# A layer-norm tail rebuilt: means from one scaled ScalarE pass, single tiles, two banks for the last tile, final steps on ScalarE and GpSimd

## The reference

```
h = gelu(x @ Wd + bd) @ Wu + bu          # 512 -> 256 -> 512
h = x + h
mean = h.mean(-1); var = ((h - mean)**2).mean(-1)
out = (h - mean) * rsqrt(var + 1e-5) * g + b   # g, b: rows of the sequence's expert
```

## Time and profile before

| | |
|---|---|
| median of 3 runs | 1041.93 us (1040.11 to 1042.93) |
| profiled execution | span 1039.0 us, from the first to the last instruction; the profile gives no other time of its own, and the median is 2.93 us above this span |
| busy share | PE 99%, PE weight loads 83%, DVE 76%, ACT 50%, POOL 1% |
| last matmul of the run starts | 1032.12 us |
| the last two stores are issued | from 1035.76 us |

### The profile page before, as it was taken

The page is one execution under the profiler, slowest core; times in us unless marked ns, Lnnn a source line. Parts: engine busy times, 40 slices in busy tenths (PEclk is TensorE's granted clock), DMA queues, the critical chain, the costliest instruction groups (busy, mean ns, idle before and its releaser), DMA issues.

```text
span 1039.0 us, 13809 instructions
## 1 busy us (share of the span) xinstructions
PE 1028.9 (99%) x4857; PEld 859.5 (83%) x4857; DVE 792.5 (76%) x1380; ACT 524.4 (50%) x955; POOL 7.5 (1%) x18
## 2 busy tenths in 40 slices
PE   8999999999999999999999999999999999999997
PEld 7899888888888878888889888888888887888886
DVE  5647957767598898887966796677668889887798
ACT  4336875454265443433565487554435644434357
POOL 0000000000000000000000000000000000000001
PEclk9999999999999999999999999999999999999999
DMA  8340211210133272521644122312004322423152
GB/s 205 60 183 21 95 48 41 82 41 21 61 144 121 101 201 83 159 85 49 238 120 118 58 68 82 122 41 81 21 21 162 142 81 104 157 98 109 41 163 81
DMA packets 91006, 101.61 MB, mean 98 GB/s; under 512 B 36830, under 2 KB 71738, under 8 KB 87098
## 3 DMA queue, kind: packets, MB, share of 16 engines
q1 hardware_dynamic: 90848, 100.71, 29.8%
q10 hardware_dynamic: 90, 0.02, 0.0%
HBM read 79.74 MB, written 20.97 MB: 97 GB/s over the span
## 4 chain that ended last, share of the span: by engine, by line
PE 59%; DVE 3%; ACT 1%; issue 1%; DVEq 0%; ACTq 0%
PE bank L224 20%; PE bank L225 20%; PE bank L226 20%; DVE acc L1124 0%; PE bank L462 0%; DVE z_last L1281 0%; DVE w_lo L1018 0%; DVE z_last L1290 0%; ACT gel L833 0%; DVE xp2l L1018 0%; ACT acc L810 0%; DVE hid_lo L1018 0%; ACT xp3h L586 0%; ACT e3h L586 0%; PE bank L376 0%
## 5 line engine op out<-in xcount | busy, mean ns | idle before, releaser
L224 PE MATMUL bank<-hid_hi,w_lo 128*128 128x512 f32 x512 | 200.3, 391 | 0.3
L676 ACT ACTIVATE sbc<-sbc,bias 128x512 f32<-128x512 f32 x112 | 80.5, 724 | 236.0 <-DVE sbc L1099 174.4
L225 PE MATMUL bank<-hid_hi,w_hi 128*128 128x512 f32 x512 | 199.3, 389 | 0.0
L226 PE MATMUL bank<-hid_lo,w_hi 128*128 128x512 f32 x512 | 199.2, 389 | 0.0
L1124 DVE TENSOR_TENSOR acc<-bank,acc 128x512 f32<-128x512 f32 x224 | 153.6, 686 | 50.9 <-PE bank L226 50.4
L224 PE MATMUL bank<-ta_hi,w_lo 128*128 128x512 f32 x448 | 174.8, 390 | 0.0
L226 PE MATMUL bank<-ta_lo,w_hi 128*128 128x512 f32 x448 | 174.4, 389 | 0.0
L225 PE MATMUL bank<-ta_hi,w_hi 128*128 128x512 f32 x448 | 174.3, 389 | 0.0
L1099 DVE TENSOR_TENSOR sbc<-bank,sbc 128x512 f32<-128x512 f32 x144 | 98.1, 686 | 38.8 <-PE bank L226 38.6
L586 ACT ACTIVATE sbc<-bank 128x512 f32<-128x512 f32 x112 | 66.4, 595 | 112.7 <-PE bank L226 112.5
L1018 DVE TENSOR_TENSOR w_lo<-w_raw,w_hi 128x256 fp32r<-128x256 f32 (+1 forms) x176 | 93.6, 562 | 37.0 <-ACT w_hi L586 37.0
(11 more groups left out here) (224 smaller groups left out, 1532.4 us busy)
## 6 DMA issues: line engine op xcount, KB each, us to landing
w_raw<-in_L_cond_mW SPq DMA_DIRECT2D x48, 512.0 KB, 3.4
w_raw<-in_L_cond_cW SPq DMA_DIRECT2D x32, 512.0 KB, 4.4
pre_d<-sbc SPq DMA_DIRECT2D x10, 1024.0 KB, 3.9
sbc<-pre_d SPq DMA_DIRECT2D x10, 1024.0 KB, 7.3
x_blk<-in_x SPq DMA_DIRECT2D x64, 64.0 KB, 2.3
e_raw<-in_L_cond_W_down SPq DMA_DIRECT2D x8, 512.0 KB, 4.5
e_raw<-in_L_cond_W_up SPq DMA_DIRECT2D x8, 512.0 KB, 4.1
proj_hi<-aw_hi SPq DMA_DIRECT2D x2, 1024.0 KB, 10.2
```

The source lines that it names most:

```text
L224: nc.tensor.matmul(dst, w_l, a_h, start=start, stop=False, **kw)
L225: nc.tensor.matmul(dst, w_h, a_h, start=False, stop=False, **kw)
L226: return nc.tensor.matmul(dst, w_h, a_l, start=False, stop=stop, **kw)
L676: nc.scalar.activation(dst, dst, ACT.Gelu, **kw).then_inc(g_done[key], 1)
```

## The change

Seven edits, all in the last layer's end. (1) ACT's first pass multiplies by -1/512 and accumulates straight into `nmean`; the Copy is gone. (2) PE works pair 3 by single tiles. (3) Tile (1,3) goes to two banks, 3 and 4, its left 256 columns in one and its right 256 in the other, with twelve matmuls of 256 columns in place of six of 512. (4) DVE takes the statistics of that tile by halves, and centres and finishes it by halves. (5) Tiles (0,2) and (1,2) get their last step elsewhere: ACT multiplies by rstd (`act_scale`), POOL adds b (`finish`). (6) `veps` and `rstd` have a column of their own for each of these tiles, and the DVE order becomes (0,2), (0,3), (1,0), (1,1), (1,2), (1,3). (7) SP stores (0,3) ahead of (0,2); the right half of (1,3) is stored from ACT's queue, the left half and then (1,2) from SP's.

```diff
+                split = n == 2 * NBAT - 1 and t == TT - 1
+                if split:
+                    pe.wait_ge(z_cent, 4 * n - 3)
                 for k in range(KT):
+                    bank = ps[LAST_BANK[k // 2]] if split else ps[b0 + t]
...
+                halves = tuple(zip(LAST_BANK, (0, V // 2), (V // 2, V)))
+                for bank, c0, c1 in halves if n == 2 * NBAT - 1 and t == TT - 1 else ((b0 + t, 0, V),):
+                    for m in range(MT):
+                        w = slice(m * V + c0, m * V + c1)
+                        last = mm3(ps[bank][:, c0:c1], ...)
+                    last.then_inc(up_mm, 1)
+            if n == 2 * NBAT - 1:
+                groups = tuple((t,) for t in range(TT))
...
+        def act_scale(act, pp, t):
+            n = 2 * NBAT - 2 + pp
+            act.wait_ge(z_cent, 4 * n + t + 1)
+            act.wait_ge(rstd_done, R_NO[(pp, t)])
+            nc.scalar.activation(z_tile(n, t), z_tile(n, t), ACT.Identity, scale=rstd_last[:, column(pp, t)])\
+                .then_inc(scaled, 1)
...
-                nc.scalar.activation(sjunk[:, c, 0, :], bank, ACT.Identity, accum_out=ssum[:, col]).then_inc(sum_done, 1)
-                act.wait_ge(sum_done, c + 1)
-                nc.scalar.activation(nmean[:, col], ssum[:, col], ACT.Copy, scale=-1.0 / V).then_inc(nmean_done, 1)
+                nc.scalar.activation(sjunk[:, c, 0, :], bank, ACT.Identity, scale=-1.0 / V,
+                                     accum_out=nmean[:, col]).then_inc(nmean_done, 1)
...
+                if c >= 2 and c != 3:
+                    act_scale(act, 0 if c == 2 else 1, 2)
...
             act_expert_last(act)
+            act.wait_ge(half_done, 2)
+            store_last(act, 1, TT - 1, RIGHT)
...
+            for t in (0, 1):
                 dve_eps_last(dve, 1, t)
                 dve_cent_last(dve, 1, t)
                 dve_out_last(dve, 1, t)
+            dve_half_stats(dve, 0)
+            dve_eps_last(dve, 1, 2)
+            dve_cent_last(dve, 1, 2)
+            dve_half_stats(dve, 1)
+            dve_aggr_last(dve, TT - 1)
+            dve_cent_halves(dve, TT - 1)
+            dve_out_last(dve, 1, 3, LEFT)
+            dve_out_last(dve, 1, 3, RIGHT)
...
+            def finish(c, pp, t):
+                n = 2 * NBAT - 2 + pp
+                pool.wait_ge(scaled, c)
+                nc.gpsimd.tensor_tensor(z_tile(n, t), z_tile(n, t), ln_p[n][:, t // TS, 1, :], ALU.add).then_inc(pool_done, 1)
+            power(0, 2)
+            power(0, 3)
+            power(1, 0)
+            finish(1, 0, 2)
+            power(1, 1)
+            power(1, 2)
+            power(1, 3)
+            finish(2, 1, 2)
...
+            sp.wait_ge(half_done, 1)
+            store_last(sp, 1, 3, LEFT)
+            sp.wait_ge(pool_done, 2)
+            store_last(sp, 1, 2, FULL)
```

More of the change, by code:

```diff
@@ L95, in build @@
         mhalf = sb("mhalf", [P, TT])
-        ssum = sb("ssum", [P, 2 * TT])
+        stat_last = sb("stat_last", [P, 2, 6])
+        veps_last = sb("veps_last", [P, 2 * TT])
+        rstd_last = sb("rstd_last", [P, 2 * TT])
         nmean = sb("nmean", [P, 2 * TT])
@@ L203, in build @@
             "max_done", "nmax_done", "rinv_done", "probs_done"))
-        sum_done, nmean_done, ssq_done = sem("sum_done"), sem("nmean_done"), sem("ssq_done")
+        nmean_done, ssq_done, half_done, pool_done = (sem(n) for n in ("nmean_done", "ssq_done", "half_done", "pool_done"))
+        scaled = sem("scaled")
         st_done, ag_done, ve_done, rstd_done, z_cent = (sem(n) for n in (
@@ L460, in token_tile @@
                 pe.wait_ge(xb_done, 4 * n + 4)
+                split = n == 2 * NBAT - 1 and t == TT - 1
+                if split:
+                    pe.wait_ge(z_cent, 4 * n - 3)
                 for k in range(KT):
-                    nc.tensor.matmul(ps[b0 + t][:, k * P:(k + 1) * P],
-                                     acc[:, k, pp * TB + t * P:pp * TB + (t + 1) * P], ident[:, :],
-                                     is_transpose=True, start=k == 0, stop=True, skip_group_check=True)
+                    bank = ps[LAST_BANK[k // 2]] if split else ps[b0 + t]
+                    nc.tensor.matmul(bank[:, k * P:(k + 1) * P], acc[:, k, pp * TB + t * P:pp * TB + (t + 1) * P],
+                                     ident[:, :], is_transpose=True, start=k == 0 or split and k == 2, stop=True,
+                                     skip_group_check=True)
             def up_tile(t):
@@ L470, in up_tile @@
                 pe.wait_ge(e_l, 8 * bb + E_RANK[bb][4 * pp + 2 + s] + 1)
[L471 to L477, removed]
+                halves = tuple(zip(LAST_BANK, (0, V // 2), (V // 2, V)))
+                for bank, c0, c1 in halves if n == 2 * NBAT - 1 and t == TT - 1 else ((b0 + t, 0, V),):
+                    for m in range(MT):
+                        w = slice(m * V + c0, m * V + c1)
+                        last = mm3(ps[bank][:, c0:c1], t_hi3[:, m, tok], t_lo3[:, m, tok], u_hi[:, s, w],
+                                   u_lo[:, s, w], False, True, skip_group_check=True)
+                    last.then_inc(up_mm, 1)
+            if n == 2 * NBAT - 1:
+                groups = tuple((t,) for t in range(TT))
+            elif bb + 1 < NBAT:
+                groups = (range(TT),)
+            else:
+                groups = ((0, 1), (2, 3))
+            for tiles in groups:
                 for t in tiles:
@@ L1258, in dve_norm @@
                         .then_inc(z_done[pp], 1)
-        R_TILE = ((0, 2), (0, 3), (1, 0), (1, 1), (1, 3), (1, 2))
-        R_NO = {pt: 4 * NBAT - 3 + c + 1 for c, pt in enumerate(R_TILE)}
+        L_TILE = A_STAT + ((1, 3),)
+        R_NO = {pt: 4 * NBAT - 3 + c + 1 for c, pt in enumerate(L_TILE)}
+        column = lambda pp, t: slice(TT * pp + t, TT * pp + t + 1)
         def dve_eps_last(dve, pp, t):
[L1264 to L1276, removed]
@@ new lines, in dve_eps_last, with dve_half_stats @@
+            dve.wait_ge(ssq_done, A_NO[(pp, t)] + 1)
+            nc.vector.tensor_scalar(veps_last[:, column(pp, t)], ssq[:, column(pp, t)], 1.0 / V, LN_EPS, ALU.mult, ALU.add)\
+                .then_inc(ve_done, 1)
+        FULL, LEFT, RIGHT = slice(0, V), slice(0, V // 2), slice(V // 2, V)
+        HALF = tuple(zip(LAST_BANK, (LEFT, RIGHT)))
+        def dve_half_stats(dve, h):
+            bank, cols = HALF[h]
+            dve.wait_ge(up_mm, 8 * NBAT + h)
+            nc.vector.bn_stats(stat_last[:, h, :], ps[bank][:, cols]).then_inc(st_done, 1)
@@ L1278, in dve_cent_last, with dve_aggr_last @@
+        def dve_aggr_last(dve, t):
+            seen = 8 * NBAT - 6
+            dve.wait_ge(st_done, seen + 2)
+            nc.vector.bn_aggr(mv[:, t, :], stat_last[:, :, :]).then_inc(ag_done, 1)
+            dve.wait_ge(ag_done, seen + 1)
+            nc.vector.tensor_scalar_add(veps_last[:, column(1, t)], mv[:, t, 1:2], LN_EPS).then_inc(ve_done, 1)
         def dve_cent_last(dve, pp, t):
             n = 2 * NBAT - 2 + pp
-            mean = nmean[:, TT * pp + t:TT * pp + t + 1] if (pp, t) in A_NO else mv[:, t, 0:1]
@@ L1281, in dve_cent_last @@
[L1281 to L1286, removed]
+            nc.vector.scalar_tensor_tensor(out=z_tile(n, t), in0=ps[(0 if pp else 4) + t][:, :], scalar=nmean[:, column(pp, t)],
+                                           in1=ln_p[n][:, t // TS, 0, :], op0=ALU.add, op1=ALU.mult).then_inc(z_cent, 1)
@@ new lines, in dve_cent_halves, with out_last @@
+        def dve_cent_halves(dve, t):
+            n = 2 * NBAT - 1
+            for bank, cols in HALF:
+                nc.vector.scalar_tensor_tensor(out=z_tile(n, t)[:, cols], in0=ps[bank][:, cols], scalar=mv[:, t, 0:1],
+                                               in1=ln_p[n][:, t // TS, 0, cols], op0=ALU.subtract, op1=ALU.mult)\
+                    .then_inc(z_cent, 1)
+        def out_last(engine, pp, t, cols):
+            n = 2 * NBAT - 2 + pp
+            return engine.scalar_tensor_tensor(out=z_tile(n, t)[:, cols], in0=z_tile(n, t)[:, cols],
+                                               scalar=rstd_last[:, column(pp, t)], in1=ln_p[n][:, t // TS, 1, cols],
+                                               op0=ALU.mult, op1=ALU.add)
@@ L1287, in dve_out_last @@
+        def dve_out_last(dve, pp, t, cols=FULL):
             n = 2 * NBAT - 2 + pp
             dve.wait_ge(rstd_done, R_NO[(pp, t)])
[L1289 to L1292, removed]
+            dve.wait_ge(z_cent, 4 * n + t + (2 if cols is RIGHT else 1))
+            out_last(nc.vector, pp, t, cols).then_inc(z_done[pp] if cols is FULL else half_done, 1)
@@ L1310, in dve_norm_last @@
-            for t in (3, 2):
+            dve_eps_last(dve, 0, 2)
+            dve_cent_last(dve, 0, 2)
+            dve_eps_last(dve, 0, 3)
+            dve_cent_last(dve, 0, 3)
+            dve_out_last(dve, 0, 3)
+            dve.wait_ge(ln_in[1], 64 * NBAT)
+            for t in (0, 1):
                 dve_eps_last(dve, 1, t)
-            for t in (2, 3):
```

(34 more changed lines are left out.)

14 lines of the change are left out of this document (1 added, 13 removed).

## The result

The changed kernel takes 1042.87 us (median of 21 runs, 1041.43 to 1043.88) against 1041.51 for the kernel before (21 runs, 1039.77 to 1042.93): ratio 1.0014, 95% interval 1.0008 to 1.0020. It is slower by 0.14% (the medians lie 1.36 us apart), where 0.3 us less was forecast. The profiled execution has a span of 1040.1 us and took 1041.87.

The account below looks back on a forecast made before the run. PE, busy 99% of the 1039.0 us span, bounds the run; only DVE's tail could move. Of 1.5 us off DVE some 0.6 remained, the last add and stores left 0.3: span 1038.7, median 1041.6, range 1040.1 to 1043.8.

Parts of the forecast that it names:

- the forecast case: Whole kernel: span 0.3 us shorter, at 1038.7, median 1041.6; chance 0.48.
- rival A: Last tiles: POOL's add shuts out DVE's final steps reading two SBUF tensors; span 1040.3, median 1043.2; chance 0.34.
- DVE's load: DVE's last tiles: two final steps fewer, halves added; 1.5 us less work, some 0.6 left after waits for ACT.
- Copy: ACT's statistics passes: without it, squaring starts 0.71 after summing instead of 0.95; a tile costs 1.39 instead of 1.63.
- POOL's add: POOL's bias add on (0,2) and (1,2), 128x512 with two inputs: taken as 1.2 us, shown by no row.
- The second way to the end: Kernel's end: POOL's add on (1,2) ends at 1035.95, 0.13 later than the right half, and sets the end.
- Rival B: POOL's add takes 1.9 us, delaying (1,1)'s power and all behind it; span 1039.9, median 1042.8; chance 0.08.
- ACT waits: DVE waits 0.3 us for ACT's sum of squares before (0,3), and 0.3 before (1,1).
- Rival C: Nothing gained: ACT's scaled pass or SBUF reads are slower and waits eat the rest; 1041.9; chance 0.10.
- Scaling pass: ACT's multiplication of (0,2) by rstd, reading SBUF with a pointer column, costs 0.63 us.
- PE: PE's last pair by single tiles, last tile in halves: the split costs nothing, but would with DVE a microsecond earlier.
- Halves on VectorE: Last tile's statistics, centring and final step by halves: three extra starts of 0.15 each, 0.45 us on.

Follow-up runs that it names:

- e2: Changed kernel with GpSimd's two adds replaced by memsets of 1472 columns of unused memory; span 1039.2 us, 17.57 from ScalarE's last-pair bias pass to the end.
- e3: Changed kernel with tiles (1,0) and (1,3) centred in place in their PSUM banks; span 1038.1 us, ratio 0.9991 to the kernel before.
- m1: Kernel before with 200 adds of 128x128 on GpSimd from 580.4 us on; span 1044.7 us.
- e7: e3 with GpSimd's second add on (1,1) instead of (1,2), (1,2) centred in its bank and finished by VectorE, stores by readiness; ratio 0.9995 to the kernel before.
- e8: e6 with SP's last stores in the order in which they are ready; span 1039.5 us, 18.24 from ScalarE's last-pair bias pass to the end.
- e6: Changed kernel with VectorE doing (0,2)'s and (1,2)'s final steps, no ScalarE scaling or GpSimd add; span 1039.3 us, 18.68 from last-pair bias pass to end.

## Why the prediction was wrong

The median fell in the range and in the band of no measurable change at 0.3%, but the direction was wrong, and the forecast case with it; rival A, given 0.34, is what happened.

The step that failed is in *DVE's load*, "(1,0): ... final step 1029.72, free 1030.39", and the same step for (1,3), "left half at 1034.94, right at 1035.34". Both priced a final step at its length from the kernel before, though each now runs beside an instruction that the trace before never had beside it. Measured: 1.66 instead of 0.75, and 1.83 instead of 0.87. I had named the meeting as rival A and priced it as 1.3 us, span 1040.3 (measured 1.30 and 1040.1), and given it less weight because no row showed it. That the two figures agree so well is luck: rival A has VectorE done at 1037.75, 16.69 after the bias pass, where 1035.29 + 1.83 - 1020.86 = 16.26 was measured, and the end 2.55 after that, where it was 2.98. The two errors, 0.43 each, cancel. A trace in which the two never overlap says nothing against an exclusion. The rule of the Trainium skill (SBUF — State Buffer, section Who interferes with whom), that a VectorE instruction with two SBUF inputs contends with a GpSimd instruction that reads SBUF and not with one that only writes it, stood beside it. The runs agree, for `scalar_tensor_tensor` too: 1.66 us beside the add, 0.75 beside e2's memset, 0.75 with one input in PSUM (e3); and either engine is held by the other (m1).

Everything else in the sum can be read from e3, where nothing is excluded. Forecast, from the bias pass at 1021.06: VectorE done after 14.76, GpSimd's add after 14.89, tail 17.64. Measured in e3: 14.64, 14.93 and 17.61.
- *Copy*: 0.71 from summing to squaring forecast, 0.70 measured; the immediate scale costs nothing.
- *POOL's add*: 1.2 forecast between 0.86 and 1.62, 1.29 and 1.26 measured; it sets the end, as forecast in *The second way to the end*. Rival B is out, though the power of (1,1) starts directly behind the add in e3 (1028.98 + 1.29 against 1030.32).
- *ACT waits*: 0.3 and 0.3 forecast, 0.28 and 0.16 measured. Rival C is out: the waits are no longer than forecast, and VectorE ends 0.70 earlier than before (15.34 to 14.64; 0.58 forecast).
- *Scaling pass*: 0.63 forecast, 0.61 measured.
- *PE*: the halves cost nothing there, as forecast. That they would cost with VectorE earlier is not borne out: in e7 the wait of 0.46 ends with the left half, whose last matmul starts at 1030.36, and the tile's last one starts 0.72 later, at 1031.08; for an unsplit tile VectorE would have had to wait for that.
- *Halves on VectorE*: 0.45 forecast, 0.33 read from e8.
- *Stores*: I had (1,2) ready after both halves, and in e3 it is. In the changed kernel it is ready at 1035.18 + 1.26 = 1036.44, but SP issues the left half first, at 1036.75, so the last 512 KB are one burst. The same order cost 0.44 in e6 against e8, and rival A has no price for it; in the changed kernel itself no run had the order turned.
- *The six other parts by themselves*: my expectation for e6 had them worth next to nothing; e6 shows a loss of 0.74, of which 0.30 is left in e8 with the stores in the other order.
- *From span to median*: I carried 2.93 over as if it were a constant. In the runs that have both on record, time and span of one execution differ by 1.74 to 1.87; the rest is that the profiled execution lay about 1.1 below the median of its kernel. The direction does not hang on it.

## What to carry to other kernels

Before work is moved from VectorE to GpSimd, list for the time of each GpSimd instruction what VectorE runs beside it, and count the SBUF inputs of both; if VectorE reads two and GpSimd reads as well, the move buys a wait (0.91 and 0.96 us in the two meetings here). Leaving one operand in PSUM took the whole loss away here with no instruction more. A blocked instruction shows no wait: compare durations within one form. Let a queue issue its stores in the order in which they become ready. And when runs scatter, find a point in the trace up to which kernels do the same, and measure from there.

## What the hardware showed that was not expected

- A `scalar_tensor_tensor` that starts 0.18 us behind a GpSimd add is held for 0.91 us of the 1.11 that the add still runs, and is recorded as busy for 1.66 us.
- Centring in place in PSUM and finishing from there cost VectorE nothing: 0.75 us each at 128x512, against 0.74 for centring into SBUF and 0.75 for finishing from it.
- A GpSimd add of 128x128 takes 0.40 us and of 128x512 1.26 to 1.29, so, by these two sizes, an estimate of 2.3 ns a column with 0.11 fixed; a power of one column takes 0.54. The Trainium skill (GPSIMD Engine Reference, section Performance versus the Vector engine) gives 4497 ns for an add of 2048 columns, 2.2 ns a column; the estimate from these runs would give 4.8 us there, 6% more.
- The span of one and the same kernel differs from run to run (1037.9 to 1041.7 us in 17 runs of the kernel before). In twelve profiles, of kernels that are the same up to the tail, the point at 542 us moves by 3.3 us, and the 478.5 us from there to the bias pass by 0.12. What makes the difference ahead of 542 us is open.
